# Attention with a norm ahead of it and a norm behind: the second norm goes from DVE to ACT, and two DVE steps change place

## What is computed

```python
x = x + xattn(layernorm(x), ctx)     # layernorm over the 512 positions, no scale, eps 1e-5
x = x + moe(layernorm(x))            # 2048 rows of 512; 16 experts, top 2, and one shared expert

# xattn: 8 heads of 16 channels, over 512 positions
q, k, v = split(xt @ w_in.T + b_in)
scores  = where(|i - j| <= 64, q k^T / 4, lowest)
o       = softmax(scores) v @ w_out.T + b_out
out     = w_ct^T (relu(o^T) * ctx) + b_ct

# moe: logits = xt @ Wr.T + bias; each row goes to its top 2 experts
y = (silu(xt Wg) * (xt Wu)) Wd
```

## Time and profile before

| what | us |
|---|---|
| median of 3 executions | 771.68 |
| the profiled execution | 771.9 |
| its span, first to last instruction | 770.2 |
| PE busy | 668.7 (87%) |
| DVE busy | 400.5 (52%) |
| ACT busy | 357.2 (46%) |
| POOL busy | 434.8 (56%) |

### The profile page before, as it was taken

How to read it: one execution, slowest core, us unless ns; L and a number is a source line. 1 busy time by engine, 2 the same in 40 slices (tenths; PEclk the granted TensorE clock), 3 DMA queues, 4 the chain that set the end, 5 groups by cost and what they waited for, 6 DMA issues and landing times.

```text
span 770.2 us, 13963 instructions
## 1 busy us (share of the span) xinstructions
PE 668.7 (87%) x4136; PEld 327.3 (43%) x4136; DVE 400.5 (52%) x1439; ACT 357.2 (46%) x672; POOL 434.8 (56%) x640
## 2 busy tenths in 40 slices
PE   3378989999999999988899895889999999999992
PEld 1235545555555555554445343433333333333330
DVE  3488788888888888762224367333222222222220
ACT  3237666666666666555323110124444444444441
POOL 2567688788777777656310000115775767757752
PEclk9579899999999999998999997999999999999997
DMA  9723334433333343211396920434555655564520
GB/s 335 204 77 93 100 99 114 114 106 101 98 104 107 107 113 114 80 31 37 109 420 233 418 88 27 139 108 83 111 125 108 142 133 114 111 135 78 88 40 1
DMA packets 64473, 95.18 MB, mean 124 GB/s; under 512 B 18064, under 2 KB 42768, under 8 KB 62224
## 3 DMA queue, kind: packets, MB, share of 16 engines
q1 hardware_dynamic: 50048, 66.75, 27.8%
q0 software_dynamic: 9600, 18.89, 13.5%
q10 hardware_dynamic: 4752, 8.65, 3.3%
HBM read 50.99 MB, written 19.14 MB: 91 GB/s over the span
## 4 chain that ended last, share of the span: by engine, by line
PE 72%; DVE 13%; issue 5%; DMA 5%; POOL 2%; SPq 1%; ACT 1%; ACTq 0%; DVEq 0%; POOLq 0%
PE bank L757 18%; PE bank L788 9%; PE bank L585 6%; PE bank L555 5%; PE bank L571 4%; DVE bank L1140 4%; PE bank L635 4%; PE bank L737 3%; PE bank L744 3%; PE bank L776 3%; PE bank L721 2%; PE bank L612 2%; PE bank L768 2%; DMA rows<-xn_rows 2%; PE bank L597 2%
## 5 line engine op out<-in xcount | busy, mean ns | idle before, releaser
L1140 DVE CUSTOM_DVE_ANT_0 bank<-bank,cb 128x192 f32<-128x192 f32 (+1 forms) x512 | 186.9, 415 | 53.2 <-PE bank L555 51.7
L927 ACT ACTIVATE wgu<-bank 128x384 f32<-128x384 f32 (+1 forms) x256 | 125.3, 544 | 57.6 <-PE bank L571 57.0
L757 PE MATMUL bank<-wgu,rowsT 128*64 x320 | 145.9, 598 | 2.8 <-DVE X L1394 2.3
L759 PE MATMUL bank<-X,rowsT 128*64 128x512 f32 x320 | 145.9, 598 | 0.0
L1379 DVE TENSOR_TENSOR act_in<-act_in,bank 128x256 f32<-128x256 f32 x56 | 23.6, 421 | 216.0 <-ACT act_in L1029 215.9
L555 PE MATMUL bank<-wgu 96*128 96x192 bf16 (+1 forms) x512 | 95.6, 272 | 21.3 <-DMA wgu<-wgu 11.7
L441 POOL TENSOR_SCALAR_AFFINE_SELECT wgu<-wgu 128x512 f32<-128x512 f32 (+1 forms) x128 | 74.5, 582 | 66.6 <-ACT wgu L927 66.2
L492 POOL DMA_INDIRECT rows<-xn_rows,gather_i x40 | 42.9, 1074 | 112.1 <-PE bank L737 93.4
L508 POOL DMA_INDIRECT out<-y_out,scatter_i x40 | 62.3, 1558 | 38.2 <-issue 22.0
L571 PE MATMUL bank<-wgu 99*128 99x192 bf16 (+1 forms) x512 | 73.8, 266 | 11.5 <-DMA wgu<-wgu 6.7
L508 POOL DMA_INDIRECT out<-y_out,scatter x40 | 61.9, 1548 | 37.0 <-DMA out<-y_out,scatter_i 17.3
(11 more groups left out here) (173 smaller groups left out, 1053.8 us busy)
## 6 DMA issues: line engine op xcount, KB each, us to landing
wgu<-wgu SPq DMA_DIRECT2D x192, 128.0 KB, 2.5
wgu<-w_gu SPq DMA_DIRECT2D x16, 1024.0 KB, 11.6
X<-w_d SPq DMA_DIRECT2D x16, 512.0 KB, 3.9
out<-y_out ACTq DMA_DIRECT2D x17, 256.0 KB, 3.6
wgu<-ctx SPq DMA_DIRECT2D x16, 256.0 KB, 3.1
xn_rows<-xn SPq DMA_DIRECT2D x16, 256.0 KB, 2.4
rows<-xn_rows ACTq DMA_DIRECT2D x16, 256.0 KB, 2.8
X<-x SPq DMA_DIRECT2D x1, 3072.0 KB, 15.3
```

The costliest lines, as they stand in the source:

```text
L757: mm(gb[k.buf][0:GROUP, :], rowsT[:, k.buf, c, 0:GROUP], wgu[:, bass.ds(e * 2048 + 512 * c, 512)], start=(c == 0), stop=(c == 3))
L759: last = mm(gb[k.buf][GROUP:P, :], rowsT[:, k.buf, c, GROUP:P], gu_half[:, k.buf, 512 * c:512 * c + 512], start=(c == 0), stop=(c == 3))
L927: nc.scalar.activation(probs[j % 4][:, 2 * half:2 * half + 2, 0:w], s2[half][:].rearrange("p (j c) -> p j c", j=2)[:, :, 0:w], ACT.Exp, sc ...
L1140: last = v.tensor_tensor_reduce(o, o, cb[:, B_MASK + off:B_MASK + off + w], 1.0, MASKED * 2.0, ALU.add, ALU.max, rowmaxes[n % 2][:, h + i, ...
```

## The change

Three edits, all in the attention part:

1. `normalise2` moves from DVE to ACT. It becomes an activation x * rstd + shift, as the first norm is, at the same offset 36, behind `first_q` and ahead of `second_q` and the exponentials in ACT's unit. For its shift, POOL's `mean_shift` runs also for the second norm (offset 35, behind `inverse_deviation`), and `shift` gets a second column.
2. `add_attention` becomes the first step of DVE's unit, ahead of the unit's first `maximum`.
3. `first_moments` is taken at offset -26 instead of -25, and `FIRST_UNIT` is -26.

```diff
-FIRST_UNIT, LAST_UNIT = -25, UNITS * (SEQS - 1) + 40
+FIRST_UNIT, LAST_UNIT = -26, UNITS * (SEQS - 1) + 40
...
-        shift = over([1])
+        shift = over([2])
...
-            def mean_shift(n):
-                pool.wait_ge(rstd1, n + 1)
-                v.tensor_scalar(shift, moments[:, 0, 0:1], rstd[:, 0:1], -1.0, ALU.mult, ALU.mult).then_inc(shift1, 1)
+            def mean_shift(which, n, rstd_sem, out_sem):
+                pool.wait_ge(rstd_sem, n + 1)
+                v.tensor_scalar(shift[:, which:which + 1], moments[:, which, 0:1], rstd[:, which:which + 1],
+                                -1.0, ALU.mult, ALU.mult).then_inc(out_sem, 1)
...
                 if (n := at(U, 35)) is not None:
                     inverse_deviation(1, n, mom2, eps2, rstd2)
+                    mean_shift(1, n, rstd2, shift2)
...
+            def normalise2(n):
+                act.wait_ge(shift2, n + 1)
+                if n >= 1:
+                    act.wait_ge(xn_stored[(n - 1) % 3], 16 * ((n - 1) // 3 + 1))
+                after(act, xt_mm, n)
+                nc.scalar.activation(xn2[:], X[:, n, :], ACT.Identity, bias=shift[:, 1:2],
+                                     scale=rstd[:, 1:2]).then_inc(xn2_ready, 1)
...
                     first_q(n)
+                if (n := at(U, 36)) is not None:
+                    normalise2(n)
                 if (n := at(U, -11)) is not None:
                     second_q(n)
...
-            def normalise2(n):
-                dve.wait_ge(rstd2, n + 1)
-                if n >= 1:
-                    dve.wait_ge(xn_stored[(n - 1) % 3], 16 * ((n - 1) // 3 + 1))
-                after(dve, xt_mm, n)
-                v.tensor_scalar(xn2[:], seq(n), moments[:, 1, 0:1], rstd[:, 1:2],
-                                ALU.subtract, ALU.mult).then_inc(xn2_ready, 1)
...
             def step(U):
+                if (n := at(U, 33)) is not None:
+                    add_attention(n)
                 if p := piece(U, -1):
                     maximum(*p, 0)
...
-                if (n := at(U, 33)) is not None:
-                    add_attention(n)
...
-                if (n := at(U, 36)) is not None:
-                    normalise2(n)
-                if (n := at(U, -25)) is not None:
+                if (n := at(U, -26)) is not None:
                     first_moments(n)
```

More of the change, by code:

```diff
@@ L245, in xattn_moe_kernel @@
             sem(s) for s in ("stats1", "mom1", "eps1", "rstd1", "shift1", "xn1_ready"))
-        stats2, mom2, eps2, rstd2, xn2_ready = (sem(s) for s in ("stats2", "mom2", "eps2", "rstd2", "xn2_ready"))
+        stats2, mom2, eps2, rstd2, shift2, xn2_ready = (
+            sem(s) for s in ("stats2", "mom2", "eps2", "rstd2", "shift2", "xn2_ready"))
         q_mm, k_mm, v_mm = sem("q_mm"), sem("k_mm"), sem("v_mm")
@@ L461, in step @@
                     inverse_deviation(0, n, mom1, eps1, rstd1)
-                    mean_shift(n)
+                    mean_shift(0, n, rstd1, shift1)
                 if (n := at(U, 30)) is not None:
@@ L892, in normalise1 @@
                 after(act, v_mm, n - 2)
-                nc.scalar.activation(xn1[n % 3], X[:, n, :], ACT.Identity, bias=shift,
+                nc.scalar.activation(xn1[n % 3], X[:, n, :], ACT.Identity, bias=shift[:, 0:1],
                                      scale=rstd[:, 0:1]).then_inc(xn1_ready, 1)
+            def normalise2(n):
[5 more added lines that the diff above has]
+                                     scale=rstd[:, 1:2]).then_inc(xn2_ready, 1)
             def first_q(n):
```

## The result

The changed kernel takes **778.35 us** (median of 20 runs, 774.36 to 785.60), the kernel before beside it 773.90 (20 runs, 770.54 to 778.38): 1.0063 [1.0044, 1.0081], slower by 0.6%. I had said 768.0, with 763.0 to 773.0 as the range. Sign and range are wrong. By the ratio the loss is 4.9 us, small but clear of the interval.

A forecast was written before the change was run, and what follows sets the result against it. Loop A (DVE and TensorE) was taken to set the 20.30 us period, with loop B close under it. Nine periods -1.5, drain -1.8 and first moments -0.4 gave -3.7 us, from median 771.68 to 768.0; range 763.0 to 773.0.

The forecast's parts named there:

- The steady period: Distance between successive sequences' query projections in the attention part: to fall from 20.30 to 20.13 us.
- slot 3: Units with U mod 8 = 3; TensorE's wait there for the maxima's DMA was to grow from 0.5 to about 1.2 us.
- the clock rival: Slower: slot 3's wait drops TensorE to 1.2 GHz every period, 1.5 us each, up to 781.8 us; chance 0.12.
- the gathered wait: TensorE's waits of slots 1 and 3 collected before the shifted scores in slot 3, about 1.2 us.
- The norm on ACT: Second norm in slot 4 ahead of ACT's exponentials: +0.33 us a period on loop B, bounds +0.2 to +0.54.
- loop A: DVE and TensorE chain from slot 1's addition to the output's norm; sets 20.30 us, to become 19.4.
- loop B: Chain of POOL, SP, maxima's DMA, TensorE and ACT: 19.80 us alone, 20.13 after the change.
- POOL's shift: One more 128x1 operation on POOL in slot 3, 0.27 us, covered by idle time: costs nothing.
- the first moments: Statistics moved from slot 7 to slot 6: nothing in steady periods, -0.4 us in all while the pipeline fills.
- The drain: Two last periods of attention, without query projection: each starts 0.9 us earlier, -1.8 us in all.
- The clock was not won back: Rival: without the drain's waits TensorE stays at full clock there, giving 764.8 us; chance 0.17.
- One for one: The expert part starts when attention ends, so its start was carried over by the same amount.

The follow-up runs named there:

- after: The changed kernel with all three edits, unedited, against the kernel before: ratios 1.0063 and 1.0061.
- the fillers: Six 128x512 matmuls nobody reads, ahead of TensorE's slot 3 wait from the fifth sequence on; alone on the kernel before: 774.84 us, 1.0028.
- after_fill: The changed kernel with six filler matmuls in slot 3 from the fifth sequence on: 774.00 us, 1.0025.
- no_add: The changed kernel with the addition put back behind the maximum of its unit: 780.37 us, 1.0070.
- add_fill: The kernel before with the addition first and six filler matmuls from the fifth sequence on, run twice: 770.44 us, 0.9944 and 770.42 us, 0.9961.
- act_dummy: The kernel before with DVE's norm kept and ACT doing the second norm again into a buffer nobody reads: 1.0036.
- norm_only: The kernel before with only the second norm on ACT and POOL's shift for it: 778.51 us, 1.0024.
- dve_shift: The kernel before with the second norm still on DVE, but computed as x*rstd + shift with POOL's shift: 1.0002.
- add_norm: The changed kernel with the moments put back, so addition first and norm on ACT: 775.99 us, 1.0014.
- after_4: The changed kernel unedited, run again in the fourth group of experiments for a third trace: 780.07 us.
- the first group: Follow-up kernels on one chip testing the edits alone and the clock; the changed kernel, unedited, took 779.24 us there, 1.0061.
- mom_only: The kernel before with only the first moments one unit sooner: 774.81 us, 0.9996.
- fill6: The changed kernel with six filler matmuls ahead of the slot 3 wait from the first sequence on: 775.67 us, 0.9999.
- add_only: The kernel before with only the addition first in DVE's unit: 775.84 us, 1.0006.

## Why the prediction was wrong, point by point

**The steady period: right where the clock holds.** I said 20.13; it is 19.8 to 20.1 over the three traces of the changed kernel. The wait of L612 is gone, L597 waits no longer, slot 3 has all of the waiting, at 1.35 where I said about 1.2. That the maxima's DMA is late next was right. (One reading is off a little: I had the start of POOL's slot 5 one period earlier by subtraction, at 197.23, and the timeline has 197.35.)

**The step that failed: the chance of the clock rival, and its all-or-nothing form.** I had the mechanism, the place (the gathered wait at L571 in slot 3), the undecided stretch of 1.04 to 1.43 us and a price of 1.5 us a period, and gave it 0.12. What held me back was the point against, that TensorE may already wait in slot 2; it doesn't: nothing of the sort is in the waits of after. I also priced it as "in every period" although my own sum had three periods as the break-even. The three traces show 10.3, 10.3 and 19.9 us at 1.2 GHz, and nine periods of 183.6, 183.0 and 186.8 us; 20.05 nine times are 180.5. So a fall of some 3.4 us costs 1.0 to 1.3 us, about a third of its length, and the changed kernel pays 2.5 to 6.4 us for gains of 2.2.

That the falls are a cause, and not a companion, four kernels show: the addition in front alone 1.0006, the fillers alone 1.0028, both together 0.9944 and 0.9961. In the changed kernel the fillers take 1.0061 to 0.9999, or to 1.0025 in after_fill, where one fall is left and the first four sequences have none; the interval of the latter overlaps that of the changed kernel a little.

The falls are not all of the miss. With the clock held the changed kernel is at 0.9999 and 1.0025, and not at the 0.995 of my forecast; and no_add loses 0.7% without them. From add_fill to after_fill it is 0.64 to 0.81%, 5 to 6 us; the norm's 0.30 in nine periods gives 2.7 of them, and the one fall left in after_fill (21.78 against 19.95) 1.8. A rest of 1 us is inside the intervals; the 0.7% of no_add is more than its parts, and stays open.

**The norm on ACT: the size was right, the cover was not.** +0.33 a period was my figure; 0.20 alone, 0.30 with the clock held (19.95 against 19.65). act_dummy shows it to be ACT's 0.80 us in slot 4. But norm_only lost its 0.20 under a loop A that should have hidden it, so the two loops are not apart as I drew them: both run through slot 3's wait and the query projection. And add_fill's 19.65 lies under the 19.80 that I took for loop B alone.

**POOL's shift and the first moments: nothing, about right.** dve_shift has the shift and stays at 20.30. The moments were to give 0.4 us; alone they give nothing (0.9996), with fillers +0.8 us, both inside the intervals. Without fillers, the kernels with the moments and the norm took more than the sum (no_add 1.0070 against norm_only 1.0024, after 1.0061 against add_norm 1.0014). No trace shows where; this stays open.

**The drain: right.** -1.8 forecast; over three traces each, it went from 124.3 to 122.9, -1.5, in one execution 123.3 with no edit at all. The clock was not won back, with 10 to 14 us at 1.2 GHz behind 300 us in each of the six traces: the wait in slot 3 grew there too, as the point against that rival said.

**What I left out: the expert part.** "One for one" took no account of a part whose blocks depend on where two engines' long operations meet. It adds 1.9 us in the three traces of each (240.9 to 242.8), 1.5 over all of them.

**The sum.** The time up to the first of the nine periods is unchanged (111.4 and 111.1 in the mean of three). An execution near the median of the changed kernel, after_4 by its time, then has +4.1 in the nine periods (186.8 - 182.7), -1.4 in the drain and about +1.9 in the experts: +4.6, against 4.7 and 4.9 by the two ratios. Routing and the tail differ by +1.6 and -1.3 and nearly cancel. This leans on one trace for the first term; in the mean of the three traces it is +1.8, and the whole comes to 2.2 us, since two of the three are of the fastest runs. So the sum is fitting and not proof. What supports it beyond that trace is the mean granted clock over all runs of the first group: 0.943 for the changed kernel (12 runs) and 0.956 for the kernel before (35). At 1.2 GHz instead of 2.4 the clock counts half, so the time at the lower level is 2 x 0.057 x 779 = 89 us and 2 x 0.044 x 775 = 68: 20 us more, which is after_4's 19.9 and not the 10 of the two other traces. That support is weak as well: the mean is of the whole execution, and in the traces the time at 1.2 GHz in the first 60 us alone goes from none (no_add, mom_only) to 40 us (fill6).

The Trainium skill (Perfetto Trace Analysis, Optimizing Scalar/DVE Operations), by whose rule an operation with a DVE performance mode is better left there unless DVE is saturated, was on the right side; in which mode the norm ran no trace shows. The rows agree: 0.59 us on DVE became 0.80 on ACT, DVE has room in slot 4, and every kernel with ACT's norm has a higher ratio than its partner without it, though for add_norm (1.0014 against 1.0006) the intervals can't tell the two apart.

## What to carry to other kernels

Before you free an engine from two short waits, ask where the waiting goes: two waits of 1.0 and 0.5 us that the clock survives can be worth as much as one of 1.35 that it doesn't (add_only, 1.0006). When a trace shows the clock at 1.2 GHz behind such a wait, try to cover it with matmuls that nobody reads; here that turned an edit worth nothing into -0.4 to -0.6%, and gained nothing where the clock had not fallen. And take a second trace of the unedited kernel before explaining a difference between two traces: the expert part's 3 to 5 us were in the kernel before as well.

## What I had not expected of the hardware

Behind waits of 1.17, 1.28 and 1.37 us the clock fell and behind one of 1.46 it did not, in one trace; falls came in two to five of nine like periods, in add_only in nearly every second one, and in four of the five traces that have them behind this wait never in two periods running. POOL's scatter issue takes up to 1.50 us alone and up to 2.49 when DVE's 128x2048 copy lies in it or across its edge, with no semaphore between the two. The Trainium skill (Trainium Architecture — The Big Picture, What this means for kernel authors) names a port that DVE and GpSimd share and that one of them locks; the rows agree in part: 2.36 us with the copy inside at block 15, but in other blocks 1.40 with a copy wholly inside, so something else decides too, and what was not found. And moving 0.8 us of ACT work in the attention part goes with a lengthened scatter of block 15 in eight of eight traces, some 200 us later.
